# Order and queue of the stores and item loads in a chunked delta-rule and mixture-of-experts layer

## What is computed

```
h = embeddings[x]
h = h + attn(layernorm(h))
    k, q, v = short_conv(x @ W.T + b)              # four taps along the tokens
    k, q normalized per head; v = silu(v); beta = sigmoid(x @ Wbeta.T + bbeta)
    per chunk:  T = tril(Bi @ Ki.T, -1)            # "Gram"; Bi = beta * k
                Ui = inv(I + T) @ (Vi - Bi @ W_t)
                W_new = W_t + Ki.T @ Ui            # and W_avg, a weighted mean
                O_i = Qi @ W_avg * a + Qi @ W_t * c + T_mat * (Qi @ Ki.T) @ Ui
    out = rms_norm(O) @ Wout.T + bout
h = h + ffn(layernorm(h))                          # top 2 of 8 experts, and the shared one
```

## Time and profile before

| | before |
|---|---|
| median of three runs | 1499.64 us (1498.28 to 1503.63) |
| profiled execution, its own time | 1499.78 us |
| its span, first to last instruction | 1498.0 us |
| mean granted TensorE clock | 0.877 |
| TensorE busy | 1181.4 us (79%) |
| VectorE busy | 762.3 us (51%) |
| ScalarE busy | 516.6 us (34%) |
| GpSimd busy | 390.3 us (26%) |
| SyncE's queue (q1) | 194.28 MB, 45.8% of 16 engines over the span |

### The profile page before, as it was taken

How to read it: one execution, slowest core, us unless ns; L and a number is a source line. 1 busy time by engine, 2 the same in 40 slices (tenths; PEclk the granted TensorE clock), 3 DMA queues, 4 the chain that set the end, 5 groups by cost and what they waited for, 6 DMA issues and landing times. The chain is left out here.

```text
span 1498.0 us, 28824 instructions
## 1 busy us (share of the span) xinstructions
PE 1181.4 (79%) x10846; PEld 795.5 (53%) x10846; DVE 762.3 (51%) x1707; ACT 516.6 (34%) x1049; POOL 390.3 (26%) x366
## 2 busy tenths in 40 slices
PE   4855465666666564787688988999999999999997
PEld 2643344353535352566466764665566666666664
DVE  4699959586868685478547873122111121111111
ACT  3454245453636261234152323331122222222221
POOL 6100123131112021533136004661022222222222
PEclk9878778787888785578788988999999999999999
DMA  7754557768695869688687748952122232323222
GB/s 265 195 125 125 129 165 171 225 149 245 136 255 120 253 134 267 200 244 246 172 256 230 222 129 338 346 167 78 28 47 47 45 48 43 47 47 46 47 46 30
DMA packets 237366, 228.68 MB, mean 153 GB/s; under 512 B 88980, under 2 KB 177972, under 8 KB 236080
## 3 DMA queue, kind: packets, MB, share of 16 engines
q1 hardware_dynamic: 202944, 194.28, 45.8%
q0 software_dynamic: 16368, 19.96, 7.7%
q10 hardware_dynamic: 17920, 12.59, 2.8%
HBM read 117.39 MB, written 115.62 MB: 156 GB/s over the span
## 5 line engine op out<-in xcount | busy, mean ns | idle before, releaser
L1683 DVE TENSOR_TENSOR hid_all<-p_s,silu 128x512 f32<-128x512 f32 x103 | 71.2, 691 | 379.4 <-PE p_s L1534 249.7
L1733 POOL DMA_INDIRECT out_h<-y_sb,x_in x71 | 110.5, 1557 | 360.9 <-DVE y_sb L1695 338.4
L1591 ACT ACTIVATE silu<-p_m 128x512 f32<-128x512 f32 x103 | 61.6, 598 | 328.0 <-PE p_m L1527 223.3
L801 DVE SCALAR_TENSOR_TENSOR cv<-raw,conv_sb,cv 128x512 f32<-128x512 f32 x144 | 116.5, 814 | 84.6 <-ACT raw L696 83.6
L172 DVE TENSOR_TENSOR prod<-nx,xt 128x62 f32<-128x62 f32 (+15 forms) x248 | 139.3, 562 | 2.5
L175 DVE TENSOR_TENSOR xt<-xt,prod 128x62 f32<-128x62 f32 (+15 forms) x248 | 138.4, 558 | 4.3
L290 PE MATMUL p_item<-xbd,bv_i 128*32 128x128 f32 x1024 | 48.1, 347 | 110.5 <-DMA xbd<-chunk_inverse_dram 37.6
L1549 PE MATMUL p_y<-wo,hid_all 128*128 x568 | 134.4, 379 | 0.8 <-ACT hid_all L1608 0.8
L1527 PE MATMUL p_m<-wi,xT_c 128*128 x284 | 133.6, 592 | 0.5 <-ACT xT_c L1604 0.5
L1534 PE MATMUL p_s<-ws,xT_c 128*128 x284 | 133.6, 593 | 0.0
L574 PE MATMUL p_p<-xT,wqkv_sb 128*128 128x512 f32 x192 | 108.7, 706 | 0.7 <-ACT xT L688 0.7
(11 more groups left out here) (155 smaller groups left out, 2124.4 us busy)
## 6 DMA issues: line engine op xcount, KB each, us to landing
slots_in_dram<-xt SPq DMA_DIRECT2D x18, 520.0 KB, 5.5
x_in<-slots_in_dram SPq DMA_DIRECT2D x71, 130.0 KB, 2.1
q_channels_dram<-qT SPq DMA_DIRECT2D x128, 64.0 KB
k_tokens_dram<-h SPq DMA_DIRECT2D x32, 256.0 KB
chunk_gram_dram<-h SPq DMA_DIRECT2D x32, 256.0 KB, 4.4
beta_kv_dram<-h SPq DMA_DIRECT2D x8, 1024.0 KB
nx<-chunk_gram_dram SPq DMA_DIRECT2D x8, 1024.0 KB, 6.3
scores_dram<-h SPq DMA_DIRECT2D x8, 1024.0 KB
```

Of the source, the lines that this page charges most:

```text
L801: ins = dve.scalar_tensor_tensor(cv[:, p, m, :], raw[:, p, m, j:j + L], conv_sb[:, p, m, j:j + 1], cv[:, p, m, :], ALU.mult, ALU.add)
L1683: dve.tensor_tensor(dst, p_s[n % 2][:], silu[n % 2][:], ALU.mult).then_inc(S["hid_ready"], 1)
L1733: pool.indirect_dma_start(token_rows, bass.IndirectOffsetOnAxis(x_in[s % X_IN][:, D:D + 1].bitcast(U32), 0), y_sb[s % 2][:], None, compute ...
```

## The change

q is laid out in DRAM as channels by tokens and stored in eight transfers of 128 KB with runs of 2 KB (a q load then has runs of 512 B). z of an item is stored in one transfer instead of four. The stores of `bv`, scores and k are issued by ScalarE, at the places shown. SyncE's order in a batch becomes: z and queries of item r-1, scores and q of r+1, `move_item(r+1)`, the inverses, `move_item(r+2)`, q stores, x of item r+4, y of r+3, z and queries of r+2, first Gram stores, scores and q of r+4, last Gram stores, x of r+5, y of r+4, `nx`.

```
-    qT_dram = nc.dram_tensor("q_channels_dram", [B, TILES, P, HQ, P], F32, kind="Internal").ap()
+    qT_dram = nc.dram_tensor("q_channels_dram", [B, HQ, P, L], F32, kind="Internal").ap()
-        STORES = 16 * (16 + 2)
+        STORES = 16 * (8 + 2)
-            sp.dma_start(q_i[:], qT_dram[b, t]).then_inc(s_q_in, 16)
+            sp.dma_start(q_i[:], qT_dram[b, :, :, t * P:(t + 1) * P].rearrange("n p l -> p n l")).then_inc(s_q_in, 16)
-            for c in range(CH):
-                sp.dma_start(zo_dram[t * CH + c, b], zo_out[i][tok(c)].rearrange("p w h d -> p (w h d)")
-                             ).then_inc(s_zo_st[i], 16)
+            sp.dma_start(zo_dram[t * CH:(t + 1) * CH, b], zo_out[i][:].rearrange("p w h d -> p (w h d)")).then_inc(s_zo_st[i], 16)
@@ sync @@
                     if b >= AHEAD:
-                        move_item(sp, r)
+                        if r:
+                            store_rest(sp, r - 1)
+                        load_scores(sp, r + 1)
                         move_item(sp, r + 1)
                     if b >= 2:
                         store_inverse(sp, b - 2)
                     if b >= AHEAD:
                         move_item(sp, r + 2)
                     sp.wait_ge(s_nrm, b * 4 + 4)
-                    for f in range(4):
-                        for m in range(2):
-                            for w in range(2):
-                                sp.dma_start(qT_dram[b, :, f * C + w * DH:f * C + (w + 1) * DH, m::2].rearrange("t d n l -> d n t l"),
-                                             qT[m * 4 * DH + f * DH:m * 4 * DH + (f + 1) * DH].rearrange("d n (t l) -> d n t l", t=TILES)
-                                             ).then_inc(s_st, 16)
-...
+                    for n in range(HQ):
+                        for w in range(2):
+                            sp.dma_start(qT_dram[b, n].rearrange("(f w d) l -> w f d l", w=2, d=DH)[w],
+                                         qT[n % 2 * 4 * DH:(n % 2 + 1) * 4 * DH, n // 2]).then_inc(s_st, 16)
+                    if b == AHEAD - 1:
+                        load_x(sp, 0)
+                        load_scores(sp, 0)
+                    if b >= AHEAD:
+                        load_x(sp, r + 4)
+                        store_y(sp, r + 3)
+                        store_rest(sp, r + 2)
                     for half in range(2):
                         sp.wait_ge(s_ng, b * TILES + 2 * half + 2)
...
-                        if half == 0:
-                            sp.wait_ge(s_bv, b * 4 + 4)
-                            sp.dma_start(bv_dram[b].rearrange("(t p) x -> p t x", p=P),
-                            if b >= AHEAD:
-                                move_item(sp, r + 3)
+                        if half == 0 and b >= AHEAD:
+                            load_scores(sp, r + 4)
+                    if AHEAD - 1 <= b < B - 1:
+                        load_x(sp, r + 5)
+                        store_y(sp, r + 4)
                     sp.wait_ge(s_ngst, 64 * (b + 1))
                     sp.dma_start(nx[b % 2][:] ...
-                    sp.wait_ge(s_sT, b * TILES + TILES)
-                    sp.dma_start(sT_dram[b].rearrange("(t p) x -> p t x", p=P), ...
@@ scalar @@
+                def store_beta_kv(b):
+                    act.wait_ge(s_bv, b * 4 + 4)
+                    act.dma_start(bv_dram[b] ...).then_inc(s_st, 16)
+                def store_scores(b):
+                    act.wait_ge(s_sT, b * TILES + TILES)
+                    act.dma_start(sT_dram[b] ...).then_inc(s_st, 16)
+                def store_k(b):
+                    act.wait_ge(s_kt, b * 2 + 2)
+                    act.wait_ge(s_ktri, b * TILES + TILES)
+                    for c in range(CH):
+                        act.dma_start(kk_dram[:, b] ...[c], kk[tok(c)] ...).then_inc(s_kst, 16)
                     item(b - 1, 3, scored_out, 0)
                     item(b - 1, 3, inner_out, 1)
+                    if b:
+                        store_beta_kv(b - 1)
                     for n in range(6):
...
                             item(b, 0, scored_out, 0)
+                            if b:
+                                store_scores(b - 1)
...
                     item(b, 3, solved_out, 0)
+                    store_k(b)
                     item(b, 3, turned_out, 1)
                 item(B - 1, 3, scored_out, 0)
                 item(B - 1, 3, inner_out, 1)
+                store_beta_kv(B - 1)
+                store_scores(B - 1)
```

More of the change, by code:

```diff
@@ L340, in turned_out @@
             if r >= 2:
-                act.wait_ge(s_zo_st[r % 2], 16 * CH * (r // 2))
+                act.wait_ge(s_zo_st[r % 2], 16 * (r // 2))
             act.copy(zo_out[r % 2][:, 0], bank[:].rearrange("p (h w d) -> p h w d", w=2, d=DH)[:, :, 1, :]).then_inc(T["z_ready"], 1)
@@ L485, in sync @@
                             start_next(sp)
-                        if half == 0:
-                            sp.wait_ge(s_bv, b * 4 + 4)
-                            sp.dma_start(bv_dram[b].rearrange("(t p) x -> p t x", p=P),
-                                         bv[:].rearrange("p t h w d -> p t (h w d)")).then_inc(s_st, 16)
-                            if b >= AHEAD:
-                                move_item(sp, r + 3)
+                        if half == 0 and b >= AHEAD:
[3 more added lines that the diff above has]
+                        store_y(sp, r + 4)
                     sp.wait_ge(s_ngst, 64 * (b + 1))
@@ L494, in sync @@
                                  n_dram[b].rearrange("g (c i) x -> (g c) (i x)", i=C)).then_inc(s_nx, 16)
-                    sp.wait_ge(s_sT, b * TILES + TILES)
-                    sp.dma_start(sT_dram[b].rearrange("(t p) x -> p t x", p=P),
-                                 sT[:].rearrange("p t g x -> p t (g x)")).then_inc(s_st, 16)
-                    if b == AHEAD - 1:
-                        load_x(sp, 0)
-                        load_scores(sp, 0)
             def gpsimd(pool):
@@ L680, in item @@
                         step(act, TILES * (b - AHEAD) + k, p_i[bank])
+                def store_beta_kv(b):
+                    act.wait_ge(s_bv, b * 4 + 4)
+                    act.dma_start(bv_dram[b].rearrange("(t p) x -> p t x", p=P),
+                                  bv[:].rearrange("p t h w d -> p t (h w d)")).then_inc(s_st, 16)
+                def store_scores(b):
+                    act.wait_ge(s_sT, b * TILES + TILES)
+                    act.dma_start(sT_dram[b].rearrange("(t p) x -> p t x", p=P),
+                                  sT[:].rearrange("p t g x -> p t (g x)")).then_inc(s_st, 16)
+                def store_k(b):
+                    act.wait_ge(s_kt, b * 2 + 2)
+                    act.wait_ge(s_ktri, b * TILES + TILES)
+                    for c in range(CH):
+                        act.dma_start(kk_dram[:, b].rearrange("(t c) i x -> c i t x", c=CH)[c],
+                                      kk[tok(c)].rearrange("p t h w d -> p t (h w d)")).then_inc(s_kst, 16)
                 act.wait_ge(s_w, 16 * 7)
@@ L975, in load_step @@
                     sp.wait_ge(s_y_st[t % 2], 16 * done)
-                    sp.wait_ge(s_zo_st[t % 2], 16 * CH * done)
+                    sp.wait_ge(s_zo_st[t % 2], 16 * done)
                     sp.wait_ge(s_qy_st[t % 2], 16 * done)
```

## The result

The changed kernel takes 1486.84 us (median of 19 runs, 1478.15 to 1498.92), the kernel before 1501.56 in 19 runs beside it (1495.34 to 1506.50, and one run at 1716.83 that stands by itself). The ratio is 0.9908 (95% interval 0.9888 to 0.9928): some 14 us faster, where 31.6 were forecast. The direction held, and the late item loads were indeed the limit; less than half of the forecast size came.

The account below looks back on a forecast made before the run. The prediction took SyncE's queue as the limit, in its issue time and the bytes ahead of a load. 1499.8-14.6 (batch 3)-15.6 (batches 4 to 7)-3 (second stage)+1 (ScalarE) gave 1468 us, range 1436 to 1508.

Parts of the forecast that it names:

- all sixteen engines: Rival: all sixteen DMA engines carry the new q and z stores; 1441 us (1425 to 1455), chance 0.26.
- second stage: Entry to the second stage: x loads go ahead; gain 3 us narrow (-6 to 8), 12 wide, of 13.1 waited.
- narrow form: New q and z stores run on four engines: 11.9 us per MB each, 70.4 us of work a batch; chance 0.44.
- Gain 54.6-38 = 16.6; I take 15.6: Batches 4 to 7: VectorE's copy waits fall from 54.6 to 38 us; 15.6 taken, as some backlog is carried on.
- q issue time 11.27 to 5.6: SyncE's queue: eight q stores at 0.70 us each instead of sixteen; x of item 0 issued 13.4 us earlier.
- Item 0's wait should go: TensorE's wait of 7.3 us before item 0's inverse product ends, as its x is issued 13.4 us earlier.
- Item 1's x issued by T+2.5: SyncE issues it from T, the end of a batch's last scores on VectorE, to T+2.5, 6 us earlier.
- nx hides: The nx load, now behind item 1's x and y, is wanted only over 20 us later, so its delay is hidden.
- Queries and z of the previous item are pushed behind nx too; nobody on the path waits for them: SyncE's queue: these stores come later than nx, at no cost to the critical path.
- ScalarE's issues hidden: ScalarE's six new issues and three waits a batch hide behind other waits, except in batch 1: +1 us in all.
- Given back: Rival: gaps in the four engines' work keep batches at 77.4 us, only batch 3 gains; 1499 us, chance 0.15.
- Slower: Rival: four engines set the period, a batch takes 83 us; 1518 us, chance 0.15.

Follow-up runs that it names:

- e6: The changed kernel with both old forms of the q and z stores, keeping the new order and queues; 0.9712 of the kernel before.
- e1: The changed kernel with q stored in sixteen transfers and z in four, spread over sixteen engines; 1455.3 us, 0.9689 of the kernel before.
- e10: The changed kernel with item 0's x loaded ahead of the narrow q stores; 0.9922 of the kernel before.
- e13: e3 with a third buffer for z during the first stage; 0.9838 of the kernel before.
- e14: The changed kernel, both narrow forms, with a third buffer for z; 0.9874 of the kernel before.
- e8: e1 with the four k stores of a batch issued by SyncE again; 0.9687 of the kernel before.
- e12: e1 with all of ScalarE's stores (k, beta-k/v, scores) given back to SyncE; 0.9794 of the kernel before.
- e5: The changed kernel with z in four transfers and q in sixteen 64 KB transfers of outermost count 2; 1.0002 of the kernel before.
- e15: e10 with a third buffer for z; 0.9921 of the kernel before.
- e3: The changed kernel with only q stored in sixteen transfers over sixteen engines, z still narrow; 0.9816 of the kernel before.
- e9: e3 with z and queries of an item issued behind the next item's loads of scores and q; 0.9870 of the kernel before.
- e11: e1 with eight stores of the inverse in the second stage issued behind item 23's loads; 0.9697 of the kernel before.

## Why the prediction was right and wrong, step by step

**The bound, right.** The late item loads on SyncE's queue were the limit: e6, which changes only their order and the stores' queue, takes VectorE's waits from 73.2 to 23.6 us and 2.9% off the time. The third stage did not move (592.7 and 593.2 us).

**The size: two terms failed that the forecast and its rival "all sixteen engines" share.** Here are the terms, as the prediction has them and as the traces of the changed kernel and of e1 (built to be that rival) give them, in us gained:

| term | forecast, narrow | changed kernel | forecast, wide | e1 |
|---|---|---|---|---|
| batch 3 | 14.6 | 12.3 | 15.6 | 15.3 |
| batches 4 to 7 | 15.6 | 8.0 | 32.6 | 24.2 |
| second stage | 3 | -4.7 | 12 | 4.2 |

Batches 4 to 7 fall short by 7.6 and 8.4 us, the second stage by 7.7 and 7.8, whether the stores are narrow or wide. The price of the narrow form, the difference between the two forecasts, was 27 us; the ratios give 33, and the three rows above 28.1, nearly row by row.

**"Gain 54.6-38 = 16.6; I take 15.6" for batches 4 to 7, the step that failed.** The waits of VectorE for copies came as forecast: 36.3 us in these four batches against 38 (21.9 in e1 against 22). But the step took waits saved for time saved. The 38 was to hold later norms and ScalarE's issues as well, which the copy waits alone used up: the norm waits rose from 6.5 to 12.6 us. And VectorE's busy time, put at no change without a reason, rose from 237.1 to 244.4 us for the same 449 instructions. Of the 18.3 us of copy waits saved these two take 13.4; with 3.1 us less of other idle time, 8.0 are left. In e1 they take 6.5 and 3.7 of 32.7, and 24.2 are left, 1.7 of them from other idle time. Why VectorE is busy longer is open. The narrow stores are not the whole of it: e6, with wide ones, is busy 310.8 us in the five batches, more than the changed kernel's 304.8.

**q issue time 11.27 to 5.6, wrong.** The eight stores took 5.92 us in one batch (from 377.22), but 11.86 and 11.93 in those before and after it; over all of them, in ns, minimum, median and maximum of one are:

```profile
L470 SPq DMA_DIRECT2D q_channels_dram<-qT x64: 503/961/2989, 50.5 to 535.6; - x64
```

The sum took an issue as a fixed price per instruction. It is that only while the engines keep up: in the quiet place 16 stores of one size take 11.0 us on sixteen engines and 17.3 on two. Item 0's x was to go out 13.4 us earlier; from the start of the q stores it went out after 11.98 us in the batch shown (19.07 before), so 7.1 earlier.

**"Item 0's wait should go", wrong for the change, right without the narrow stores.** The waits before the product of item 0 of each of the five batches were 3.6, 1.5, 10.6, 1.0 and 4.3 us; in e1 they are 0, 1.6, 0.4, 1.7 and 0. The issue did come earlier, but the bytes landed late, in batch 5 9.8 us after it. Half of these waits did go (the four in batches 4 to 7 were 11.8, 7.2, 7.3 and 9.7 us in the kernel before), and e10, which ends the rest, gains nothing.

**Item 1's x issued by T+2.5, half wrong.** It went out at T+3.8, T+8.0, T+0.0 and T+5.1 in the four batches from 251.66 on; in e1 at T+1.9, 0.0, 0.0 and 0.0.

**"nx hides", right. "Queries and z of the previous item are pushed behind nx too; nobody on the path waits for them": wrong as worded, without consequence.** ScalarE waited for z stores 3 times, 7.1 us, and 26.5 us in e10, but e13 and e14 take such waits away and gain nothing that can be told from their errors.

**ScalarE's issues hidden, right in what they cost where it was tested.** k's four issues can take 7 us instead of 3.04:

```profile
458.67 2.29 ACTq L689 DMA_DIRECT2D k_tokens_dram<-h  x1
460.99 4.40 ACTq L689 DMA_DIRECT2D k_tokens_dram<-h  x2
465.48 0.59 ACT L337 COPY yz_tok<-p_item 128x512 f32<-128x512 f32 x1 [5.92 <-issue]
```

yet e8, without them on ScalarE, is no faster than e1. e1 and e8 have wide stores, with which k's issues on ScalarE take 2.8 to 4.1 us in e1; with narrow ones no run tests it. That queue was even underrated: the move of beta-k/v and scores brings 1.0% (e12), which the sum had priced at +1 us with no gain of its own.

**The narrow form, right in kind and nearly in size; how it costs is not shown.** The prediction took four engines, and e1 to e5 show it. Its price was 11.9 us per MB, from a dense stretch of 2 KB runs at 101.8%. In the quiet place four engines move 68 GB/s over 4 us, whose start is idle, and 78 over the last three of them, at which 1.05 MB take 15.4 or 13.4 us. So the work of the four engines in a batch is 73 to 77 us in place of 70.4, and batches 4 to 7 took 76.0 on average. That the four engines' total sets the 76 us fits this, e10, e14 and e15, but it is not shown: e3, with only z narrow, has by the same sum some 10 to 12 us less work and the same 76.0 us a batch. There part of the cost is scores loads behind z (e9: 7.0 of the 17.6 us by which e3's five batches exceed e1's); the other 10.6 stay unexplained.

**The second stage, wrong in sign, the other step that failed.** It was to give 3 us ("nearly all of the 13.1" of waits before items 20 and 21 with wide stores) and took 4.7 more. TensorE's waits there for the items' x and beta-k/v did fall, from 19.5 us to 12.9 (13.1 in e1). But its waits for the z loads of the state steps rose from 12.2 us to 31.2 (27.5 in e1). The wait moved to the next load, as in e11, and mostly did so with wide stores too. Finer differences can't be settled: kernels with nearly the same code differ by up to 10 us there (e1 and e8 at 325.3 and 319.5, e11 at 330.1), and their granted clocks differ too (0.81, 0.83 and 0.81).

**The rivals.** "All sixteen engines" was valued at 1441 (1425 to 1455); e1, built to be just that, took 1455.3, just outside the range, for the same two terms as above. "Given back" had batches of 77.4 us from gaps in the four engines' work; the changed kernel's took 76.0, and it came out between this rival (1499) and the forecast. "Slower" decided from 67.5 us of work on an engine with gaps of 10; the changed kernel's batches stayed under 77.5 on average, though batch 5 took 82.0.

## What to carry to other kernels

Before a store is merged or its runs are lengthened, look at the outermost counts on both sides: here 2 KB runs on four engines lost two thirds of what the new order had won, and the same runs split by sixteen kept it all. Do not take the waits of one group of instructions for time: here they fell just as forecast, and under half of them came back, since other waits and busy time of the same engine grew. Before a wait is priced, list what its engine waits for next, here `beta` behind item 0's x and the state's z load behind the items' loads. When removing a wait gains nothing, find where it reappears before removing the next one.

## What the runs showed of the hardware

An engine that carries part of a narrow transfer moved more than one of a wide transfer: 68 GB/s over 4.0 engines is 17 each, 51 over 2.2 is 23, 137 over 12.2 is 11. So a third of the busy engines gave half of the bandwidth. This holds for these stores and not for any wide transfer: in the dense stretch of the earlier trace rows sixteen engines moved 1.08 MB in 3 us, 22 GB/s each. The wide stores may be held back by their issue, which takes as long as the transfers here, or by small packets: of the 397 packets in e1's 4 us 130 are under 512 B, of the 132 in the changed kernel's 6. No run parts these two.

A DMA-issuing instruction is not of fixed length. One q store took 0.70 us to issue in the kernel before and 1.48 in two batches of the changed kernel, an x load's four issues 1.8 to 7.2 us, and ScalarE's k stores were held up as well as SyncE's, though the narrow stores were all SyncE's:

```profile
377.22 5.92 SPq L470 DMA_DIRECT2D q_channels_dram<-qT  x8
383.25 7.20 SPq L227 DMA_DIRECT2D xbd<-chunk_inverse_dram  x4
```

Here the q stores issued fast, and the four x loads behind them paid for it. So a time line of issues is worth a look when few engines carry much.
